# Fetching a quarter of the key rows through DRAM in the edge stage of a graph-attention and expert kernel

## The chip, the cores and the metric

The program runs on one core of a Trainium2 chip. The metric is the device time of one execution in microseconds (us). Before the change the median of three executions is 590.24 us (589.01 to 591.65). Engines are named as the profile names them: PE (TensorE), DVE (VectorE), ACT (ScalarE), POOL (GpSimd) and SP, whose queue issues plain transfers.

## The reference, cut to what matters

A layer norm, a Nystrom attention with a graph stage, and a mixture of 16 experts are computed in one launch. The change touches the graph stage alone:

```
enc = xg[0] + dense                      # only batch 0 is used: 512 tokens
q, k = enc @ wq, enc @ wk                # 32 columns each
scores = q @ k.T / sqrt(32)
contrib = adj_vals * scores[adj_rows, adj_cols]        # 16384 edges
A_raw = segment_sum(contrib, adj_rows, num_segments=n) # 512 sums
alpha = softmax(A_raw)
```

Since the score of an edge is a dot product, the kernel sums `adj_vals * k[adj_cols]` by row first (`kv` in the code), and multiplies by `q` afterwards.

## The kernel before, in words

The 16384 edges lie as 128 partitions by 128 columns, in 16 groups of 8 columns (`NG = 16`, `EG = 8`). One group takes these steps:

- VectorE makes a one-hot of the edges' columns (`one_hot_cols`, 4 instructions of 128x1024, L1204). TensorE gathers the key rows with it: 96 matmuls of 32 columns (`gather`, L2039), since `k` is held as three bf16 parts (`ksp`).
- VectorE multiplies the gathered rows in PSUM by the edge values (`product`, L1219). The result is split into three bf16 parts: ScalarE makes the first (`split_1`, L762), VectorE the residual (`middle`, L1226), ScalarE the second part (`split_2`, L766), VectorE the third (`lower`, L1231).
- The one-hot of the edges' rows is made by VectorE for 6 of 8 columns (`one_hot_rows`, L1212) and by ScalarE for 2 (`row_distances`, L773, and `last_rows`, L779).
- TensorE sums by row with 32 matmuls of 96 columns into bank 4 (`segment`, L2049).

Two slots (`s`) alternate between even and odd groups in all buffers. A loop runs 7 times over pairs of groups on PE, DVE and ACT; the last pair stands behind it. The order on each engine is the order in which the code is written, and semaphores join the engines. On DVE a group is product, one-hot of columns of the group two ahead, middle, one-hot of rows of the next group, lower. On ACT it is split_1, row_distances of the next group, split_2, last_rows of the next group. One-hot of rows for group g waits until segment g-2 has ended (`g_done`).

When the last segment has ended, a matmul of zeros (L2063) closes bank 4, VectorE forms the sums (L1255, L1258), the softmax follows, and SP starts the load of the experts' second weights. POOL does nothing in the edge stage: its last instruction before it is an iota (L551), its next waits for work far behind it. POOL is later the engine that gathers and scatters token rows for the experts, with indirect DMAs (`rows`, L602, and `results`, L610).

`kf` holds the key rows in fp32 in SBUF (L1193); L1194 to L1197 make `ksp` from it. `idx_i` and `idx_f` hold the edges' indices as integers and as floats.

Of the kernel before, what the change touches and what calls it, by code (L numbers as in the profile page):

```python
# [5 lines left out]
def sandwich_kernel(nc, dense, adj_rows, adj_cols, adj_vals, wq, wk, wv_w, wv_b, qkv_w, wq_t, wk_t, out_w, out_b,  # L6
                    conv_pad, keys_t, w1_t, b1_t, w2_t, b2, rw_t, rb, out):

    fp32 = mybir.dt.float32
# [23 lines left out]
    EG = 8  # L33
    EACT = 2
    NG = EC // EG
    QK = wq.shape[1]
    NS = 3
    E, TOPK = keys_t.shape[1], 4
# [25 lines left out]
    with ctx:  # L64
        def sb(name, shape, dt=fp32):
            return ctx.enter_context(nc.sbuf_tensor(name, shape, dt))
# [59 lines left out]
        colb = shared[:, 0:EDGE_OC].bitcast(fp16)  # L126
        oh_c = shared[:, EDGE_OC:EDGE_OR].bitcast(bf16).rearrange("p (a c n) -> p a c n", a=2, c=NT)
        oh_r = shared[:, EDGE_OR:EDGE_OR + EG * N].bitcast(bf16).rearrange("p (a j n) -> p a j n", a=2, j=EG)
        EDGE_OR1 = EDGE_OR + EG * N // 2
        qlT, klT = [shared[:, EDGE_OR1 + i * HP * B * L:EDGE_OR1 + (i + 1) * HP * B * L]  # L130
                    .rearrange("p (c n) -> p c n", c=HP) for i in range(2)]
# [42 lines left out]
        neg = sb("neg", [P, EC])  # L174
        vals = sb("vals", [P, EC])
        colT = sb("colT", [P, EC], fp16)
        col_dram = nc.dram_tensor("col_dram", [EDGES], fp16, kind="Internal").ap()

        kv, kvr = [xnT[:, i * N:(i + 1) * N].rearrange("p (a j q) -> p a j q", a=2, j=EG) for i in range(2)]
# [158 lines left out]

        def step_of(n):
            return n // JT * NI + n % JT

# [75 lines left out]
        def _(sp):  # L419
# [30 lines left out]
            sp.wait_ge(const_ready, 2)  # L450
            for i in range(BT):
                sp.dma_start(b2_bd[i * E:(i + 1) * E, i * D:(i + 1) * D], b2).then_inc(ffnc_in, 16)
            sp.wait_ge(alpha_ps, 1)
            sp.dma_start(w2_sb, w2_t).then_inc(w_in, 16)
            def store_rows(h):
# [31 lines left out]
            for i in range(IALL):  # L487
                if i == NI:
                    sp.wait_ge(exp_ready, 3)
                if first_of_group(i):  # L490
                    group = experts(sp, i)
                if i == 2:
                    sp.wait_ge(xg_in[1], 16)
                first_weights(i, group[i % NI % EB])
                if i == HOT_STEP + 12:
                    store_rows(1)
                elif i >= NI:
                    finish(i)
# [9 lines left out]
        def _(pool):  # L508
# [51 lines left out]
            iota(iota_x, [[1, P], [0, TK]], 0, 0).then_inc(const_ready, 1)  # L560


            pool.wait_ge(enc_ready, 1)
            for t in range(NT):
                if t == 0:
# [31 lines left out]
            def rows(n):  # L597
                if n >= XR:
                    pool.wait_ge(own_ready, 3 * ((n - XR) // GRP) + 1)
                if n >= XSEM:  # L600
                    pool.wait_ge(xg_in[n % XSEM], 16 * (n // XSEM))
                pool.indirect_dma_start(out=xg[:, n % XR, :], out_offset=None, in_=xd[n // JT][:, :],  # L602
                                        in_offset=bass.IndirectOffsetOnAxis(ap=idx_src[:, n:n + 1], axis=0))\
                    .then_inc(xg_in[n % XSEM], 16)
# [343 lines left out]
        def _(dve):  # L948
# [29 lines left out]
            def values(b):  # L978
                if b == 0:
                    dve.wait_ge(wv_in, 32)  # L980
                dve.wait_ge(val_ps, b + 1)
                v.tensor_tensor(out=value[:, b * NT:(b + 1) * NT, :],
                                in0=bank[2 + b % 2][:, :].rearrange("p (t d) -> p t d", t=NT),
                                in1=wvb_row[:, :].unsqueeze(1).broadcast_to([P, NT, D]), op=ALU.add)\
                 .then_inc(val_ready, 1)
# [18 lines left out]
            for b in range(1, 6):  # L1004
# [18 lines left out]
            step(v.tensor_tensor(out=idx_f[:, 1, :], in0=idx_f[:, 1, :], in1=neg[:, :], op=ALU.add))  # L1023
            v.tensor_scalar(idx_f[:, 1, :], idx_f[:, 1, :], 0.0, float(N - 1), ALU.max, ALU.min)\
             .then_inc(colT_need, 1)
            values(4)
            dve.wait_ge(xl_ps, 1)
            v.tensor_copy(xlT[:, :], bank[7][:, 0:B * L]).then_inc(xl_ready, 1)
# [184 lines left out]
                                          ALU.is_equal)  # L1213
                ins.then_inc(ohr_ready, 1)

            def product(pair, s):
                g = 2 * pair + s
                dve.wait_ge(kg_ps, 2 * pair + s + 3)
                v.tensor_tensor(out=kv[:, s, :, :],  # L1219
                                in0=bank[s][:, 0:EG * QK].rearrange("p (j q) -> p j q", j=EG),  # L1220
                                in1=vals[:, bass.ds(g * EG, EG)].unsqueeze(2).broadcast_to([P, EG, QK]),
                                op=ALU.mult).then_inc(kv_ready, 1)

# [18 lines left out]
                lower(pair, s)  # L1242

            dve.sem_inc(kv_ready, 2)
            with dve.Fori(0, NG // 2 - 1) as pair:
                group(pair, 0)
                group(pair, 1)
            group(NG // 2 - 1, 0, 1)
            group(NG // 2 - 1, 1, 0)
            enc(BH)  # L1250
            enc(BH + 1)

# [513 lines left out]
        def _(pe):  # L1766
# [285 lines left out]
                ins.then_inc(g_done, 1)  # L2052

            gather(0, 0)
            with pe.Fori(0, NG // 2 - 1) as pair:
                gather(pair, 1)
                segment(pair, 0)
                gather(pair + 1, 0)
                segment(pair, 1)
            gather(NG // 2 - 1, 1)  # L2060
            segment(NG // 2 - 1, 0)
            segment(NG // 2 - 1, 1)
            mm(bank[4][:, 0:NT * NS * QK], zeros[:, 0:P], zeros[:, 0:NT * NS * QK], start=False, stop=True,  # L2063
               skip_group_check=True).then_inc(alpha_ps, 1)
            idle(3, 7)
# [98 lines left out]
                    bias_rows(4 + (j - 4) // 2)  # L2164

            def rows_T(n):
                pe.wait_ge(xg_in[n % XSEM], 16 * (n // XSEM + 1))
                freed(pe, xgT_ready, n - 1)
                nc.tensor.transpose(bank[n % 2][:, 0:P], xg[:, n % XR, 0:D], ident[:, :]).then_inc(xgT_ps, 1)  # L2169

# [92 lines left out]
```

## Time and profile before

| | |
|---|---|
| median of three executions | 590.24 us |
| the profiled execution | 585.99 us, span 584.3 us |
| PE, DVE, ACT, POOL busy | 86%, 61%, 60%, 48% of the span |
| edge stage, first gather to last segment | 89.1 to 160.5 us |
| mean granted clock of TensorE | 0.929 of 2.4 GHz |

The profiled execution is 4.25 us below the median of the three timed ones, so sums over its rows are made against 585.99 us and their difference is then carried to 590.24 us. The span is the time between the first and last instruction. An engine's busy share over the whole span is a mean over stages with different limits: in the edge stage POOL is idle altogether.

### The profile page before, as it was taken

To read this page: it belongs to the slowest core of one execution; us is meant where nothing else is said; L and a number is where in the kernel's file an instruction comes from. 1 tells how busy PE (TensorE), PEld (TensorE's weight loads), DVE (VectorE), ACT (ScalarE), POOL (GpSimd) and SP (SyncE) were. 2 spreads that over 40 slices of the span, in tenths; PEclk is the share of its full clock that TensorE was granted. 3 is DMA by queue.
4 is the path that set the end of the run, shared out by engine and by line. 5 is a ranking of instruction groups with operands and counts; after the bars stand their busy time and mean duration, and the time that the engine had idled before them with its cause. 6 is when DMAs were issued, how large, how long until landed. Compare 5 with 4: busy or idle time off the path is not lost.

```text
span 584.3 us, 18669 instructions
## 1 busy us (share of the span) xinstructions
PE 501.3 (86%) x6226; PEld 464.5 (80%) x6226; DVE 354.3 (61%) x1302; ACT 353.1 (60%) x1067; POOL 282.4 (48%) x309
## 2 busy tenths in 40 slices
PE   3989978999826056999989999999999999999963
PEld 3975868999814043999989999999998999999722
DVE  6563666999889963667587787122235664442136
ACT  5723316777574643665686998666766666666404
POOL 5000010000005615776777777777777777777700
PEclk9999996999966557999999999999999999999978
DMA  8974000000070023675667776776698977687382
GB/s 242 255 228 191 3 3 3 0 0 0 1 288 1 1 90 107 189 204 167 176 182 188 196 264 177 206 215 182 178 269 268 288 227 199 201 234 225 101 289 74
DMA packets 55738, 92.19 MB, mean 158 GB/s; under 512 B 10352, under 2 KB 26096, under 8 KB 55152
## 3 DMA queue, kind: packets, MB, share of 16 engines
q1 hardware_dynamic: 45424, 72.35, 40.9%
q0 software_dynamic: 10240, 18.89, 11.4%
q8 instruction: 42, 0.69, 0.5%
q14 instruction: 32, 0.26, 0.2%
HBM read 78.07 MB, written 17.37 MB: 163 GB/s over the span
## 4 chain that ended last, share of the span: by engine, by line
PE 65%; DVE 15%; issue 6%; ACT 6%; DMA 4%; POOL 3%; DVEq 1%; POOLq 0%; SPq 0%; ACTq 0%
PE bank L2177 23%; PE bank L2184 21%; DVE shared L1212 3%; PE bank L2169 2%; DVE shared L1204 2%; PE bank L1771 2%; PE bank L2106 2%; DMA shared<-yd 2%; DMA yd<-value_early 2%; POOL yd L610 2%; PE bank L1876 2%; PE bank L1808 1%; PE bank L1798 1%; PE bank L2039 1%; PE bank L2122 1%
## 5 line engine op out<-in xcount | busy, mean ns | idle before, releaser
L908 ACT ACTIVATE value_early<-bank,shared 128x128 f32<-128x128 f32 x632 | 180.7, 369 | 96.8 <-PE bank L2177 95.4
L2177 PE MATMUL bank<-value_early,shared 128*128 x1264 | 170.2, 278 | 4.2 <-ACT value_early L916 3.6
L2184 PE MATMUL bank<-shared,value_early 128*128 x1264 | 167.4, 275 | 2.2 <-ACT value_early L908 2.2
L2177 PEld LDWEIGHTS bank<-value_early,shared 128*128 128x128 f32 x1264 | 154.9, 193 | 7.4 <-issue 7.3
L2184 PEld LDWEIGHTS bank<-shared,value_early 128*128 128x128 f32 x1264 | 154.0, 192 | 2.6 <-issue 2.6
L602 POOL DMA_INDIRECT shared<-xd,value_early x128 | 125.5, 980 | 56.1 <-issue 31.7
L610 POOL DMA_INDIRECT yd<-value_early x128 | 126.8, 991 | 40.6 <-issue 28.7
L1695 DVE SCALAR_TENSOR_TENSOR value_early<-bank,value_early 128x128 f32 x158 | 54.8, 347 | 88.5 <-PE bank L2184 76.1
L572 POOL TENSOR_TENSOR shared<-shared,xn 128x512 f32<-128x512 f32 x4 | 5.1, 1267 | 96.3 <-DVE xn L1288 89.9
L2039 PE MATMUL bank<-ksp,shared 128*128 128x32 bf16 x1536 | 41.1, 178 | 0.0
L2039 PEld LDWEIGHTS bank<-ksp,shared 128*128 128x128 bf16 x1536 | 40.3, 97 | 0.1
L551 POOL IOTA value_early<- 128x2048 f16 x1 | 2.5, 2466 | 73.6 <-PE bank L2014 73.6
L916 ACT ACTIVATE value_early<-bank 128x128 f32<-128x128 f32 x128 | 37.6, 295 | 0.3 <-PE bank L2169 0.3
L2169 PE MATMUL bank<-ident,shared 128*128 128x128 f32 x128 | 35.5, 277 | 1.7 <-DMA shared<-xd,value_early 1.7
L2049 PE MATMUL bank<-xnT,shared 128*128 128x96 bf16 x512 | 25.8, 211 | 7.1 <-DVE xnT L1231 7.1
L1777 PE MATMUL bank<-zeros 128*128 128x512 bf16 x55 | 16.4, 461 | 17.3 <-DVE mv L1297 12.2
L2049 PEld LDWEIGHTS bank<-xnT,shared 128*128 128x128 bf16 x512 | 23.8, 101 | 8.2 <-issue 5.4
L1777 PEld LDWEIGHTS bank<-zeros 128*128 128x128 bf16 x55 | 6.0, 112 | 25.7 <-DVE mv L1297 12.3
L1212 DVE TENSOR_SCALAR shared<-iota_r,idx_f 128x512 bf16<-128x512 f16 x90 | 24.9, 346 | 1.2 <-PE bank L2049 1.2
L1678 DVE TENSOR_TENSOR value_early<-shared,mask 128x128 f32<-128x128 f32 x16 | 4.7, 292 | 33.4 <-PE bank L2169 33.4
L1204 DVE TENSOR_SCALAR shared<-shared,iota_c 128x1024 bf16 x56 | 23.3, 478 | 0.0
L2169 PEld LDWEIGHTS bank<-ident,shared 128*128 128x128 f32 x128 | 18.5, 145 | 3.5 <-DMA shared<-xd,value_early 3.0
(341 smaller groups left out, 699.7 us busy)
## 6 DMA issues: line engine op xcount, KB each, us to landing
shared<-w1b SPq DMA_DIRECT2D x158, 258.0 KB
w1b<-in_w_t SPq DMA_DIRECT2D x1, 4096.0 KB
shared<-col_dram SPq DMA_DIRECT2D x1, 4096.0 KB
shared<-in_w_t SPq DMA_DIRECT2D x1, 4096.0 KB
att<-yd SPq DMA_DIRECT2D x8, 512.0 KB, 5.7
shared<-yd SPq DMA_DIRECT2D x4, 1024.0 KB, 9.1
xd<-xnT SPq DMA_DIRECT2D x2, 1280.0 KB, 5.1
shared<-xd,value_early POOLq DMA_INDIRECT x128, 3.7
```

The source lines that it names most:

```text
L602: pool.indirect_dma_start(out=xg[:, n % XR, :], out_offset=None, in_=xd[n // JT][:, :], in_offset=bass.IndirectOffsetOnAxis(ap=idx_src[:, ...
L610: pool.indirect_dma_start(out=yd[:, :], out_offset=bass.IndirectOffsetOnAxis(ap=idx_dst[:, m:m + 1], axis=0), in_=yg[:, m % YSLOTS, :], in ...
L908: ins = act.activation(hT[:, i % 2, tok(c)], bank[2 + i % 2][:, tok(c)], ACT.Gelu, bias=w1_now[:, i % WR, F + c:F + c + 1])
L916: act.activation(xgT[:, n % SLOTS, :], bank[n % 2][:, 0:P], ACT.Copy).then_inc(xgT_ready, 1)
L1204: ins = v.tensor_scalar(oh_c[:, s, c, :], colb[:, bass.ds(g * (EG * P), EG * P)], iota_c[:, c:c + 1], None, ALU.is_equal)
L1212: ins = v.tensor_scalar(oh_r[:, s, j, :], iota_r[:, :], idx_f[:, 0, bass.ds(g * EG + j, 1)], None, ALU.is_equal)
L1695: v.scalar_tensor_tensor(out=y, in0=bank[6 + i % 2][:, 0:P], scalar=own_f[:, bass.ds(own_at, 1)], in1=y, op0=ALU.mult, op1=ALU.add).then_i ...
L2039: ins = mm(bank[s][:, j * QK:(j + 1) * QK], oh_c[:, s, c, j * P:(j + 1) * P], ksp[:, c, n, :], start=(c == 0 and n == 0), stop=(c == NT - ...
L2049: ins = mm(bank[4][:, c * NS * QK:(c + 1) * NS * QK], oh_r[:, s, j, tok(c)], kvs[:, s, j, :, :].rearrange("p n q -> p (n q)"), start=False ...
L2169: nc.tensor.transpose(bank[n % 2][:, 0:P], xg[:, n % XR, 0:D], ident[:, :]).then_inc(xgT_ps, 1)
L2177: ins = mm(bank[2 + i % 2][:, tok(c)], w1_now[:, i % WR, tok(c)], x_now, start=True, stop=True)
L2184: ins = mm(bank[6 + i % 2][:, 0:D], hT[:, i % 2, tok(c)], w2_sb[:, bass.ds(e, 1), c, :] .rearrange("p a d -> p (a d)"), start=(c == 0), st ...
```

## The change

Four of the 16 groups (`GP = 4`, groups 12 to 15) no longer get their key rows from TensorE. SP stores `kf` to DRAM (`k_dram`), VectorE converts the clamped column indices to integers, and POOL issues 32 indirect DMAs, each of which fetches 128 rows of 128 bytes into `kgp`. The four one-hots of columns and the four gathers of these groups are gone. The loop runs 5 times instead of 7, and the groups behind it are written out, with the product of a group ahead of the lower part of the group before it. ScalarE's instructions are the same. The semaphores `xg_in[0]` to `xg_in[3]` are used for the 32 DMAs too, so later waits on them count 128 more (`landed`).

```diff
+    GP = 4
+    PP = (NG - GP) // 2
...
+        kgp = early[:, 0:GP * EG * QK].rearrange("p (a j q) -> p a j q", a=GP, j=EG)
...
+        def landed(n):
+            return xg_in[n % XSEM], 16 * (n // XSEM + 1) + (16 * EG if n % XSEM < GP else 0)
...
+            sp.wait_ge(ksp_ready, 1)
+            sp.dma_start(k_dram.rearrange("(c p) q -> p c q", p=P), kf[:, :, :]).then_inc(edge_in, 16)
             sp.wait_ge(alpha_ps, 1)
             sp.dma_start(w2_sb, w2_t).then_inc(w_in, 16)
...
+            pool.wait_ge(colT_need, 2)
+            pool.wait_ge(edge_in, 64)
+            for a in range(GP):
+                for j in range(EG):
+                    at = (NG - GP + a) * EG + j
+                    pool.indirect_dma_start(out=kgp[:, a, j, :], out_offset=None, in_=k_dram[:, :],
+                                            in_offset=bass.IndirectOffsetOnAxis(
+                                                ap=idx_i[:, 1, at:at + 1].bitcast(mybir.dt.uint32), axis=0))\
+                        .then_inc(xg_in[a], 16)
             pool.wait_ge(enc_ready, 1)
...
+            dve.wait_ge(colT_need, 1)
+            v.tensor_copy(idx_i[:, 1, :], idx_f[:, 1, :]).then_inc(colT_need, 1)
...
-            def product(pair, s):
+            def product(pair, s, fetched=None):
                 g = 2 * pair + s
-                dve.wait_ge(kg_ps, 2 * pair + s + 3)
-                v.tensor_tensor(out=kv[:, s, :, :],
-                                in0=bank[s][:, 0:EG * QK].rearrange("p (j q) -> p j q", j=EG),
+                if fetched is None:
+                    dve.wait_ge(kg_ps, 2 * pair + s + 3)
+                    rows = bank[s][:, 0:EG * QK].rearrange("p (j q) -> p j q", j=EG)
+                else:
+                    dve.wait_ge(xg_in[fetched], 16 * EG)
+                    rows = kgp[:, fetched, :, :]
+                v.tensor_tensor(out=kv[:, s, :, :], in0=rows,
...
-            with dve.Fori(0, NG // 2 - 1) as pair:
+            with dve.Fori(0, PP - 1) as pair:
                 group(pair, 0)
                 group(pair, 1)
-            group(NG // 2 - 1, 0, 1)
-            group(NG // 2 - 1, 1, 0)
+            group(PP - 1, 0, 1)
+            product(PP - 1, 1)
+            middle(PP - 1, 1)
+            for a in range(GP):
+                product(PP + a // 2, a % 2, a)
+                lower(PP - 1 + (a + 1) // 2, (a + 1) % 2)
+                one_hot_rows(PP + a // 2, a % 2)
+                middle(PP + a // 2, a % 2)
+            lower(NG // 2 - 1, 1)
...
-            with pe.Fori(0, NG // 2 - 1) as pair:
+            with pe.Fori(0, PP - 1) as pair:
...
-            gather(NG // 2 - 1, 1)
-            segment(NG // 2 - 1, 0)
-            segment(NG // 2 - 1, 1)
+            gather(PP - 1, 1)
+            for a in range(NG - 2 * PP + 2):
+                segment(PP - 1 + a // 2, a % 2)
```

On VectorE behind the loop, before the change (the last two groups; the lines are product, middle, one-hot of rows, lower):

```order
183 L1219 TENSOR_TENSOR xnT<-bank,vals 128x256
184 L1226 TENSOR_TENSOR xnT<-xnT 128x256
185 L1212 TENSOR_SCALAR shared<-iota_r,idx_f 128x512 x6
186 L1231 TENSOR_TENSOR xnT<-xnT 128x8x32
187 L1219 TENSOR_TENSOR xnT<-bank,vals 128x256
188 L1226 TENSOR_TENSOR xnT<-xnT 128x256
189 L1231 TENSOR_TENSOR xnT<-xnT 128x8x32
```

The same place with the change (groups 10, 11 and the start of 12 and 13; `value_early` is where `kgp` lies; L1244 is the product, L1250 middle, L1232 the one-hot of rows, L1255 lower):

```order
184 L1244 TENSOR_TENSOR xnT<-bank,vals 128x256
185 L1250 TENSOR_TENSOR xnT<-xnT 128x256
186 L1232 TENSOR_SCALAR shared<-iota_r,idx_f 128x512 x6
187 L1255 TENSOR_TENSOR xnT<-xnT 128x8x32
188 L1244 TENSOR_TENSOR xnT<-bank,vals 128x256
189 L1250 TENSOR_TENSOR xnT<-xnT 128x256
190 L1244 TENSOR_TENSOR xnT<-value_early,vals 128x256
191 L1255 TENSOR_TENSOR xnT<-xnT 128x8x32
192 L1232 TENSOR_SCALAR shared<-iota_r,idx_f 128x512 x6
193 L1250 TENSOR_TENSOR xnT<-xnT 128x256
194 L1244 TENSOR_TENSOR xnT<-value_early,vals 128x256
195 L1255 TENSOR_TENSOR xnT<-xnT 128x8x32
```

In a fetched group the one-hot of columns is gone, and the product stands ahead of the lower part of the group before.

On TensorE, before the change, from the end of the loop to the matmul of zeros that closes bank 4:

```order
108 L2049 MATMUL bank<-xnT,shared 128x96 x32
109 L2055 REGISTER_ALU
110 L2055 COMPARE_AND_BRANCH
111 L2039 MATMUL bank<-ksp,shared 128x32 x96
112 L2049 MATMUL bank<-xnT,shared 128x96 x64
113 L2063 MATMUL bank<-zeros 128x384
```

The same place with the change:

```order
108 L2080 MATMUL bank<-xnT,shared 128x96 x32
109 L2086 REGISTER_ALU
110 L2086 COMPARE_AND_BRANCH
111 L2070 MATMUL bank<-ksp,shared 128x32 x96
112 L2080 MATMUL bank<-xnT,shared 128x96 x192
113 L2094 MATMUL bank<-zeros 128x384
```

Behind the loop stand six segments instead of two, with no gather between them.

## Rows read from the trace of the kernel before

**Rows 1.** Busy time by stretch: PE, PEld, DVE, ACT, POOL, clock, DMA.

```profile
116.00:125.00 9.00, 8.37 (x279) 8.23 (x276) 8.96 (x28) 6.75 (x12) 0.00 (x0) 1.00 0.00 0
```

**Rows 2.** Timeline of one group: start, length, engine, line, count, idle before.

```profile
118.92 0.42 DVE L1219 TENSOR_TENSOR xnT<-bank,vals 128x256 f32<-128x256 f32 x1
119.03 1.52 PE L2049 MATMUL bank<-xnT,shared 128*128 128x96 bf16 x32 [0.25 <-DVE xnT L1231]
119.26 1.67 DVE L1204 TENSOR_SCALAR shared<-shared,iota_c 128x1024 bf16 x4
119.38 0.42 ACT L762 ACTIVATE xnT<-xnT 128x256 bf16<-128x256 f32 x1 [0.92 <-DVE xnT L1219]
119.70 1.32 ACT L773 ACTIVATE xnT<-iota_r,idx_f 128x512 f16<-128x512 f16 x2
120.39 2.55 PE L2039 MATMUL bank<-ksp,shared 128*128 128x32 bf16 x96
120.84 0.42 DVE L1226 TENSOR_TENSOR xnT<-xnT 128x256 f32<-128x256 f32 x1
121.18 1.66 DVE L1212 TENSOR_SCALAR shared<-iota_r,idx_f 128x512 bf16<-128x512 f16 x6
121.62 1.13 ACT L779 ACTIVATE shared<-xnT,ones 128x1024 bf16<-128x1024 f16 x1
```

**Rows 3.** Timeline: products of groups 11 and 15, and the closing matmul.

```profile
139.99 0.41 DVE L1219 TENSOR_TENSOR xnT<-bank,vals 128x256 f32<-128x256 f32 x1
...
156.78 0.42 DVE L1219 TENSOR_TENSOR xnT<-bank,vals 128x256 f32<-128x256 f32 x1 [0.39 <-PE bank L2039]
...
160.53 0.33 PE L2063 MATMUL bank<-zeros 128*128 128x384 bf16 x1
```

**Rows 4.** Timeline: the last instruction that makes the keys' parts.

```profile
88.64 0.29 DVE L1197 TENSOR_TENSOR ksp<-kres,ksp 128x128 bf16<-128x128 f32 x1
```

**Rows 5.** DMA issues (size, us to landing); SP's waits (total, times, longest).

```profile
idx_i<-in_adj_rows SPq DMA_DIRECT2D x1, 64.0 KB, 5.8
SPq L454 <- PE bank L2063: 116.9, 1, 116.9
```

**Rows 6.** Line L602, POOL's gathers: ns min/median/max, and time to landing.

```profile
L602 POOL DMA_INDIRECT shared<-xd,value_early x128: 942/947/2028, 223.9 to 498.3; - x128
...
DMA to landing us min/median/max: 3.1/3.7/5.7
```

**Rows 7.** Timeline of DVE, then POOL, around two gathers.

```profile
342.25 1.22 DVE L1457 TENSOR_TENSOR att<-place,att 128x1024 bf16<-128x1024 f32 x1
...
342.60 1.68 POOL L602 DMA_INDIRECT shared<-xd,value_early  x1 [0.30 <-issue]
344.58 0.95 POOL L602 DMA_INDIRECT shared<-xd,value_early  x1 [0.30 <-issue]
```

**Rows 8.** Timeline of DVE, then POOL: trains of three short VectorE instructions.

```profile
348.53 1.02 DVE L1502 TENSOR_SCALAR xnT<-iota_r,att,code 128x128 f16<-128x128 f16 x3
349.21 0.42 DVE L1495 TENSOR_TENSOR xnT<-iota_r,att 128x256 f16<-128x256 f16 x1
351.79 0.76 DVE L1502 TENSOR_SCALAR xnT<-iota_r,att,code 128x128 f16<-128x128 f16 x3
352.46 0.41 DVE L1495 TENSOR_TENSOR xnT<-iota_r,att 128x256 f16<-128x256 f16 x1
...
348.58 0.97 POOL L610 DMA_INDIRECT yd<-value_early  x1 [0.30 <-issue]
```

**Rows 9.** Busy time by stretch (columns as in rows 1), the first two groups.

```profile
92.20:95.60 3.40, 2.25 (x91) 2.15 (x86) 3.40 (x11) 2.67 (x5) 0.00 (x0) 0.99 0.02 5
95.60:102.40 6.80, 5.80 (x138) 5.83 (x139) 5.48 (x18) 3.64 (x6) 0.00 (x0) 0.50 0.01 2
```

**Rows 10.** Timeline of PE: the segment of group 0.

```profile
96.60 2.72 PE L2049 MATMUL bank<-xnT,shared 128*128 128x96 bf16 x32 [2.15 <-DVE xnT L1231]
```

**Rows 11.** Line L1021: VectorE's conversion of the indices, ns min/median/max.

```profile
L1021 DVE CAST idx_f<-idx_i x1: 282/282/282, 27.2 to 27.2; 128x256 f32<-128x256 int32 x1
```

More of the change, by code:

```diff
@@ L176, in sandwich_kernel @@
         colT = sb("colT", [P, EC], fp16)
+        k_dram = nc.dram_tensor("k_dram", [N, QK], fp32, kind="Internal").ap()
         col_dram = nc.dram_tensor("col_dram", [EDGES], fp16, kind="Internal").ap()
@@ L492, in _ @@
                 if i == 2:
-                    sp.wait_ge(xg_in[1], 16)
+                    sp.wait_ge(*landed(1))
                 first_weights(i, group[i % NI % EB])
@@ L600, in rows @@
                 if n >= XSEM:
-                    pool.wait_ge(xg_in[n % XSEM], 16 * (n // XSEM))
+                    pool.wait_ge(*landed(n - XSEM))
                 pool.indirect_dma_start(out=xg[:, n % XR, :], out_offset=None, in_=xd[n // JT][:, :],
@@ L2166, in rows_T @@
             def rows_T(n):
-                pe.wait_ge(xg_in[n % XSEM], 16 * (n // XSEM + 1))
+                pe.wait_ge(*landed(n))
                 freed(pe, xgT_ready, n - 1)
```

## The prediction

> **What bounds the kernel now.** I looked first at the busy time by stretch inside the edge stage [rows 1]. In 9.00 us of the loop VectorE is busy 8.96, TensorE 8.37, ScalarE 6.75, POOL 0, at the full clock. So VectorE is the bound, TensorE is 0.6 us behind it, and POOL and the DMA rings are free. The timeline of one group then gives the terms [rows 2]: on VectorE a product of 0.42, four one-hots of columns that take 1.67, a middle of 0.42, six one-hots of rows that take 1.66, and a lower of about 0.42; a successor starts 0.34 after a start of 0.42 length, and 1.58 after the start of a block of one-hots. The period is (156.78 - 139.99)/4 = 4.20 us [rows 3]. TensorE needs a segment of 1.52 and a gather of 2.55 in it. Last I read the first two groups, since the clock is not full there [rows 9].
>
> **What is taken away.** Four gathers of 2.55 us and 16 one-hots of columns go. I count from the product of group 11, at 139.99 us. Before the change the closing matmul starts at 160.53, 20.54 us later [rows 3]. With the change the rest of the stage has ScalarE as its bound, because its work per group is unchanged: split_1 to row_distances 0.32, row_distances 1.32, split_2 to last_rows about 0.33, last_rows 1.13 [rows 2], together 3.1. VectorE needs only 0.34 + 0.34 + 1.58 + 0.34 = 2.6 per group, TensorE 1.52. Laid out: split_1 of group 11 starts 0.46 after its product (119.38 - 118.92), split_1 of group 15 at 0.46 + 4 x 3.1 = 12.9. In each group lower waits for the second split; lower of group 14 starts 0.32 + 1.32 + 0.42 + 0.05 = 2.1 after its split_1, so at 9.8 + 2.1 = 11.9. Behind it come the one-hots of rows, and middle of group 15 starts at 11.9 + 0.34 + 1.58 = 13.8. From there middle, split_2 and lower follow with 0.45 each, 0.1 to the segment, and 1.36 from the segment to the closing matmul: 13.8 + 1.35 + 0.1 + 1.36 = 16.6. The saving is 20.5 - 16.6 = 3.9 us. The product ahead of lower is part of this: it fills the wait of lower for the second split, which ends 0.05 us before it.
>
> **What is added off the path.** The store of the keys waits for the keys' last part, which ends at 88.93 [rows 4]. SP has nothing ahead of it: it waits 116.9 us for TensorE in this time [rows 5], and its next transfer, the second weights, goes out only at the end of the stage. A 64 KB transfer landed after 5.8 us in a crowded stretch [rows 5], so POOL starts at about 94.5 at the latest. VectorE's conversion costs one instruction of at most 0.28 us [rows 11]; it stands where the chain of waits runs on TensorE, and would cost 0.3 if it were not hidden. I take 0. Behind the 32 DMAs on POOL stands only work that waits for the end of the softmax. The changed counts of the expert gathers' semaphores add no instruction: 0.
>
> **Are the rows there in time?** One gather of POOL takes 0.947 us and 0.30 pass before the next [rows 6, 7]: a pitch of 1.25, so 32 x 1.25 = 40 us. A gather can be held up: the one of 1.68 us runs beside an instruction with two inputs in SBUF, L1457, which ends at 343.47; the gather ends 0.81 after that [rows 7]. In the loop VectorE is never idle, so I estimate 1.4 per gather: 94.5 + 45 = 139.5, and 3.7 to landing [rows 6] makes 143. The product of group 15 needs them at 139.99 + 10.9 = 150.9. The pitch may reach (150.9 - 3.7 - 94.5)/32 = 1.65 us before group 15 waits. The earlier groups have more room.
>
> **What POOL does to VectorE.** The trace of before has no gather beside the dense one-hots, so this is bounded. The train of short scalar compares at 348.53 is 1.02 us long, where the one at 351.79 is 0.76; the longer one ends at 349.55, exactly where POOL's DMA ends (348.58 + 0.97) [rows 8]. So the end of POOL's instruction holds back a write of VectorE by up to 0.26 us. But the instruction behind the train starts 0.68 after the train's start in one case and 0.67 in the other [rows 8]: nothing was lost. That is the lower bound, 0. The upper bound is 0.26 per gather. The nearest rows are short instructions with a pause in each; the one-hots are longer. From the blocks of 1.67/4 = 0.42 (1024 elements) and 1.66/6 = 0.28 (512 elements) [rows 2], 512 elements cost 0.14, so 0.14 of each instruction is a pause that swallows part of the hold: 0.26 - 0.14 = 0.12 lost when it strikes. The one-hots are 3.2 of 4.2 us, which makes 0.09, and since the nearest rows show none I take 0.08. Between 95.60 and 102.40 VectorE is busy 5.48 of 6.80 [rows 9], so the 6 gathers up to there are free, and 26 x 0.08 = 2.1 us are lost (bounds 0 and 26 x 0.26 = 6.8).
>
> The Trainium skill, page "SBUF — State Buffer", section "SBUF: two separate sides", says that VectorE in its two-port modes and GpSimd share a port pair by an exclusive lock, held for the whole instruction, and that GpSimd's descriptor writing starves meanwhile; the same page gives about 620 ns alone against about 3100 ns beside a VectorE copy. By the 3100 ns, an estimate from that page, the 32 gathers would take 99 us and come some 40 us late. The trace agrees that there is a lock, at the end of POOL's instruction, but not with "whole instruction": trains run within POOL's 0.97 us [rows 8].
>
> **TensorE's clock behind the loop.** With 1.52 us of work in 3.1, TensorE is busy half of the time. In the stretch 92.20 to 95.60 it was busy 2.25 of 3.40, and the clock fell to half for the next 6.8 us [rows 9]. There the segment took 2.72 us instead of 1.52 [rows 10, 2]. I expect this fall in the last four groups. The other segments hide it, since 2.72 is under 3.1; the last one is on the path: +1.2 us. Without the fall it is 0.
>
> **Sum.** -3.9 + 2.1 + 1.2 = -0.6 us. The profiled execution of 585.99 becomes 585.4. The median of the runs shown is 4.25 above it, so the forecast is 590.24 - 0.6 = 589.6. What lies behind the stage is a chain on VectorE and ScalarE that moves as a whole.
>
> **The rivals.**
> - *The gathers cost nothing.* VectorE swallows the hold as in the trains [rows 8]. Then -3.9 + 1.2 = -2.7 with the fall of the clock, -3.9 without it: 587.5 to 586.3. For it: the next start was on time. Against it: the one-hots leave a smaller pause. If what POOL takes is under 0.03 per gather and the clock holds, it is a gain of over 3 us.
> - *The whole hold is lost, and the loop's TensorE falls to the lower clock.* VectorE loses 0.26 at each of 26 gathers, 6.8 us, with the clock's 1.2: -3.9 + 6.8 + 1.2 = +4.1, 594.3. A period of 4.46 instead of 4.20 also leaves TensorE idle longer, and each fall in the loop costs at least the 1.2 us of a segment [rows 10, 2]. It is slower than before from 0.11 us per gather on. For it: the lock is there, and VectorE has no spare time. Against it: the starts in the trains.
> - *POOL is starved and the rows come late.* It gets through only about once per group, in the product, which reads PSUM. By 141 us some 11 of 32 are done; group 13 waits, and the remaining 21 go at about 1.3 behind the loop: 141 + 27 + 3.7 = 172, then 5.7 from the product of group 15 to the end, 178 against 160.5: +17, 607. It decides from a pitch of 1.65. That the change doesn't do what it says is this case. Against it: POOL's DMA was not lengthened by the train [rows 8]. By the page of the Trainium skill named above it would come out later still, as said there.
>
> **How the numbers follow.** Forecast (a loss between 0.03 and 0.2 per gather) 0.45, gathers free 0.30, whole hold 0.16, starved 0.09. I take 0.5%, 3 us, as what a measurement of this kernel can tell from no change. Faster by more than that: 0.25 of the free case (where the clock holds too, or a little more is won behind it) and 0.07 of the forecast: 0.32. Slower by more: 0.13 of the whole hold, 0.09, and 0.03 of the forecast: 0.25. Within it: 0.43. The range reaches from the free case, 586.3 less 1.0 for the spread of the medians, to the whole hold with one fall in the loop, 594.3 + 1.2: 585.3 to 595.5. It leaves out the starved case. The likeliest case alone has 587 to 593.
>
> **What would show it.** 32 DMAs on POOL between 92 and 143 us with a pitch of 1.25 to 1.5; the product of group 11 later than 139.99 by some 2 us; no wait of a fetched product for POOL or a DMA; a spacing of 3.1 between the last products, with ScalarE without idle time; a granted clock of half in the last groups, and the last segment at 2.7 us. The forecast is wrong if the product of group 11 stays at 140, if the fetched products wait for DMAs, or if POOL's instructions last over 1.5 us.

## The result, and the profile after

The changed kernel has a median of 583.56 us (582.05 to 584.30, four executions), the kernel before 589.83 beside it. The ratio is 0.9886, 95% interval 0.9854 to 0.9919: faster by 6.3 us (1.1%, clear of 1), and outside the predicted range of 585.3 to 595.5. Run twice more unchanged, it gave 0.9966 [0.9922, 1.001] and 0.9945 [0.9905, 0.9984]. Weighted by their intervals the three make 0.992, about 4.5 us; the first number was on the lucky side.

The gain is in the edge stage. I measure it from the start of the product of group 0, P0, to the start of the matmul that closes bank 4, "close". In before that is 92.20 to 160.53 [rows 3]; in the profiled execution after it is 95.07 to 158.98:

| kernel | P0 to close | P1 to P2 | P3 to P10 | P11 to close |
|---|---|---|---|---|
| before | 68.33 | 5.65 | 29.64 | 20.53 |
| before, again | 68.35 | 5.65 | 29.66 | 20.54 |
| after | 63.91 | 4.85 | 30.24 | 15.81 |
| after, again | 63.51 | 4.30 | 30.43 | 15.81 |
| after, third | 63.34 | 4.61 | 30.24 | 15.82 |

Here Pg is the start of the product of group g in us (of L1244 after, L1219 before). The stage is 4.42 us shorter in the pair of profiles: the tail gives 4.72, the steady loop costs 0.60, the first groups give 0.30. The tail repeats to 0.01 us. The spans differ by only 2.0 (584.3 and 582.3), since P0 stands 2.87 later after the change for a reason that is not the change (last section), and 0.4 is won behind the stage, where I looked for no cause.

Page of after, parts 1 and 5 (part 5: line, engine, names, count | busy us, mean ns | idle before, and what ended it):

```profile
span 582.3 us, 17846 instructions
PE 494.1 (85%) x5840; PEld 457.1 (79%) x5842; DVE 350.1 (60%) x1287; ACT 351.8 (60%) x1067; POOL 316.2 (54%) x341
L577 POOL DMA_INDIRECT value_early<-k_dram,idx_i x32 | 34.9, 1090 | 15.1 <-issue 9.4
```

POOL's 32 gathers are there, 1.09 us each. Two stretches of after, busy us of PE, PEld, DVE, ACT, POOL, then the granted clock, in the columns of [rows 1]:

```profile
113.00:122.00 9.00, 7.89 (x258) 7.78 (x259) 9.00 (x28) 6.20 (x10) 6.97 (x7) 1.00 0.15 12
144.40:155.90 11.50, 5.75 (x125) 5.33 (x123) 10.12 (x36) 11.15 (x20) 0.00 (x0) 1.00 0.01 1
```

The first answers to [rows 1]: VectorE is still never idle, and POOL is now busy 6.97 of 9.00. The second lies in the fetched groups: ScalarE is busy 11.15 of 11.50, and TensorE only half of the time, 5.75, at the full clock. Timeline of after (start, duration, engine, line; in brackets what the instruction waited for), answering to [rows 3]:

```profile
143.16 0.42 DVE L1244 TENSOR_TENSOR xnT<-bank,vals 128x256 f32<-128x256 f32 x1 [0.39 <-PE bank L2070]
153.61 0.42 DVE L1244 TENSOR_TENSOR xnT<-value_early,vals 128x256 f32<-128x256 f32 x1
157.62 1.52 PE L2080 MATMUL bank<-xnT,shared 128*128 128x96 bf16 x32 [1.30 <-DVE xnT L1255]
158.98 0.33 PE L2094 MATMUL bank<-zeros 128*128 128x384 bf16 x1
```

From the product of group 11 to the closing matmul it is 15.8 us, where before it was 20.5. The last segment is 1.52 long, not 2.72 as in [rows 10]. One fetched group of the same timeline, which answers to [rows 2]:

```profile
147.52 0.42 DVE L1250 TENSOR_TENSOR xnT<-xnT 128x256 f32<-128x256 f32 x1
147.85 0.42 DVE L1244 TENSOR_TENSOR xnT<-value_early,vals 128x256 f32<-128x256 f32 x1
148.05 0.40 ACT L784 ACTIVATE xnT<-xnT 128x256 bf16<-128x256 f32 x1
148.35 1.13 ACT L797 ACTIVATE shared<-xnT,ones 128x1024 bf16<-128x1024 f16 x1
148.48 0.43 DVE L1255 TENSOR_TENSOR xnT<-xnT 128x256 bf16<-128x256 f32 x1 [0.21 <-ACT xnT L784]
148.82 1.66 DVE L1232 TENSOR_SCALAR shared<-iota_r,idx_f 128x512 bf16<-128x512 f16 x6
149.05 1.52 PE L2080 MATMUL bank<-xnT,shared 128*128 128x96 bf16 x32 [1.36 <-DVE xnT L1255]
149.39 0.40 ACT L780 ACTIVATE xnT<-xnT 128x256 bf16<-128x256 f32 x1
149.70 1.32 ACT L791 ACTIVATE xnT<-iota_r,idx_f 128x512 f16<-128x512 f16 x2
150.40 0.42 DVE L1250 TENSOR_TENSOR xnT<-xnT 128x256 f32<-128x256 f32 x1
150.73 0.42 DVE L1244 TENSOR_TENSOR xnT<-value_early,vals 128x256 f32<-128x256 f32 x1
150.92 0.40 ACT L784 ACTIVATE xnT<-xnT 128x256 bf16<-128x256 f32 x1
```

Product to product is 150.73 - 147.85 = 2.88. ScalarE starts split_2 at 148.05, last_rows 0.30 later, split_1 1.04 later, row_distances 0.31 later, and the next split_2 1.22 after that, together 2.87, without a pause between them. VectorE has a ring that is nearly as long: middle, split_2, lower, one-hot of rows, middle (150.40 - 147.52 = 2.88 here). In group 15, where ScalarE is free, middle, split_2 and lower start at 156.15, 156.60 and 157.05, 0.45 apart; so by itself this ring would take 0.45 + 0.45 + 0.34 + 1.58 = 2.82, and ScalarE's 2.87 is the bound by 0.05. No fetched product waits for a DMA.

Last, the loop, where POOL works beside VectorE. Timeline of after:

```profile
91.83 0.40 SPq L461 DMA_DIRECT2D k_dram<-kf  x1
94.53 1.11 POOL L577 DMA_INDIRECT value_early<-k_dram,idx_i  x1 [5.70 <-DMA k_dram<-kf]
114.73 1.52 POOL L577 DMA_INDIRECT value_early<-k_dram,idx_i  x1 [0.30 <-issue]
115.36 1.79 DVE L1232 TENSOR_SCALAR shared<-iota_r,idx_f 128x512 bf16<-128x512 f16 x6
132.66 1.92 DVE L1232 TENSOR_SCALAR shared<-iota_r,idx_f 128x512 bf16<-128x512 f16 x6
137.54 1.31 POOL L577 DMA_INDIRECT value_early<-k_dram,idx_i  x1 [0.30 <-issue]
```

The store lands 2.7 us after its issue and POOL starts at 94.53; the last of 32 goes at 137.54, a pitch of (137.54 - 94.53)/31 = 1.39 us. A block of six one-hots of rows takes 1.79 or 1.92 where it took 1.66 [rows 2]: one or two of its instructions lost 0.13.

### The profile page after: what moved, and what is told of

Its sections match the earlier page's. It is cut to its first block, busy times and chain, and to the rows that moved or that the text cites. A ratio compares the mean times of both kernels' runs of the same rounds, so it can differ in the third digit from the quotient of the medians.

```text
span 582.3 us, 17846 instructions
## 1 busy us (share of the span) xinstructions
PE 494.1 (85%) x5840; PEld 457.1 (79%) x5842; DVE 350.1 (60%) x1287; ACT 351.8 (60%) x1067; POOL 316.2 (54%) x341
## 4 chain that ended last, share of the span: by engine, by line
PE 68%; DVE 14%; ACT 7%; issue 5%; DMA 3%; POOL 2%; DVEq 1%; POOLq 0%; SPq 0%; ACTq 0%
PE bank L2208 24%; PE bank L2215 22%; PE bank L2200 2%; DVE shared L1232 2%; PE bank L1802 2%; PE bank L2153 2%; PE bank L2137 2%; PE bank L1839 2%; DMA shared<-yd 2%; DVE shared L1224 2%; PE bank L1829 2%; PE bank L1907 2%; POOL yd L628 1%; PE bank L2070 1%; PE bank L2004 1%
## 5 line engine op out<-in xcount | busy, mean ns | idle before, releaser
L577 POOL DMA_INDIRECT value_early<-k_dram,idx_i x32 | 34.9, 1090 | 15.1 <-issue 9.4
L2080 PE MATMUL bank<-xnT,shared 128*128 128x96 bf16 x512 | 24.6, 207 | 13.1 <-DVE xnT L1255 13.1
L2070 PE MATMUL bank<-ksp,shared 128*128 128x32 bf16 x1152 | 31.3, 179 | 0.0
L2070 PEld LDWEIGHTS bank<-ksp,shared 128*128 128x128 bf16 x1152 | 30.6, 98 | 0.3
L1232 DVE TENSOR_SCALAR shared<-iota_r,idx_f 128x512 bf16<-128x512 f16 x90 | 26.2, 359 | 0.4 <-PE bank L2080 0.4
L791 ACT ACTIVATE xnT<-iota_r,idx_f 128x512 f16<-128x512 f16 x32 | 21.1, 707 | 0.0
```

The lines of the kernel that those rows point to most:

```text
L577: pool.indirect_dma_start(out=kgp[:, a, j, :], out_offset=None, in_=k_dram[:, :], in_offset=bass.IndirectOffsetOnAxis(ap=idx_i[:, 1, at:at ...
L1232: ins = v.tensor_scalar(oh_r[:, s, j, :], iota_r[:, :], idx_f[:, 0, bass.ds(g * EG + j, 1)], None, ALU.is_equal)
L2070: ins = mm(bank[s][:, j * QK:(j + 1) * QK], oh_c[:, s, c, j * P:(j + 1) * P], ksp[:, c, n, :], start=(c == 0 and n == 0), stop=(c == NT - ...
L2080: ins = mm(bank[4][:, c * NS * QK:(c + 1) * NS * QK], oh_r[:, s, j, tok(c)], kvs[:, s, j, :, :].rearrange("p n q -> p (n q)"), start=False ...
```

## The experiments

### POOL's part alone, and the order alone

Theory: the tail's gain comes from ScalarE's bound and POOL takes far less than 0.08 per gather. Rival: the gain has another source, and POOL's price is as forecast. The first kernel keeps the store, the conversion and the 32 gathers, and gets its groups from TensorE as before:

```diff
-            with dve.Fori(0, PP - 1) as pair:
+            with dve.Fori(0, NG // 2 - 1) as pair:
...
             for a in range(GP):
-                product(PP + a // 2, a % 2, a)
...
+                dve.wait_ge(xg_in[a], 16 * EG)
+            group(NG // 2 - 1, 0, 1)
+            group(NG // 2 - 1, 1, 0)
```

> The kernel before with POOL's part of the change alone: the store of the keys, the conversion of the indices and the 32 gathers into a buffer that nobody reads; TensorE gathers all 16 groups as before. Theory (the hold is small): POOL's gathers lengthen a group of the loop from 4.20 to about 4.30 us while they run, so 0.6 to 0.9 us in all, and the edge stage from the keys' last part (L1197 of before) to the closing matmul is 71.9 + 0.8 = 72.7 us. Rival (my forecast: 0.08 per gather): +2.1, 74.0 us. Second rival (whole hold of 0.26): +6.8, 78.7 us.

Measured: 1.0025 [0.9986, 1.0064]; P0 to close 69.49 against 68.33 at the same P1 to P2 (5.64), so POOL's part costs 1.16 us, 0.036 per gather. That is more than the 0.6 to 0.9 of the theory and about half of the 2.1 of my forecast. P3 to P10 is 30.50 (+0.86); the tail, where POOL is done, is 20.54 and unchanged.

The second keeps everything but the order of the fetched groups:

```diff
-                product(PP + a // 2, a % 2, a)
-                lower(PP - 1 + (a + 1) // 2, (a + 1) % 2)
                 one_hot_rows(PP + a // 2, a % 2)
+                lower(PP - 1 + (a + 1) // 2, (a + 1) % 2)
+                product(PP + a // 2, a % 2, a)
                 middle(PP + a // 2, a % 2)
```

> The changed kernel with the order of the parts in the fetched groups as before: one-hot of rows of the next group, lower, then the next product, then middle. Theory (in the fetched groups two chains are equally long, ScalarE's own work of 2.87 us, and middle, second split, lower, one-hot of rows): with the old order product, first split and middle stand in a row, 0.34 + 0.13 + 0.47 + 0.34 + 1.58 + 0.34 = 3.2 us per group instead of 2.87, so from the product of group 11 to the closing matmul 16.6 to 17.2 us instead of 15.8: the kernel is 0.8 to 1.4 us slower than the changed one. Rival (ScalarE alone sets the period, the order is worth nothing): 15.8 us again.

Measured: 0.9983 [0.9944, 1.0023], tail 19.28. The expectation, 3.2 us per group and 16.6 to 17.2, missed: a group takes 3.70. Timeline of this kernel:

```profile
148.25 0.42 DVE L1255 TENSOR_TENSOR xnT<-xnT 128x256 bf16<-128x256 f32 x1
148.81 1.52 PE L2080 MATMUL bank<-xnT,shared 128*128 128x96 bf16 x32 [2.18 <-DVE xnT L1255]
150.37 1.67 DVE L1232 TENSOR_SCALAR shared<-iota_r,idx_f 128x512 bf16<-128x512 f16 x6 [0.46 <-PE bank L2080]
151.95 0.42 DVE L1255 TENSOR_TENSOR xnT<-xnT 128x256 bf16<-128x256 f32 x1
158.37 2.67 PE L2080 MATMUL bank<-xnT,shared 128*128 128x96 bf16 x32 [0.48 <-DVE xnT L1255]
160.88 0.33 PE L2094 MATMUL bank<-zeros 128*128 128x384 bf16 x1
```

Here is a ring that I had not seen: lower of a group releases its segment, the segment's end (`g_done`) releases the one-hot of rows of the group two ahead, since that buffer has two slots, and the next lower stands behind these one-hots on VectorE. 0.56 + 1.56 + 1.58 = 3.70. Fetching the rows without the order gives 20.53 - 19.28 = 1.3 us; the order gives 19.28 - 15.81 = 3.5.

The 3.5 is not the ring alone. The last segment takes 2.67 us here and 1.52 in the changed kernel: TensorE's clock fell during the last group. The granted clock is 0.97 from 152.52 to 157.70, with TensorE busy 3.00 of 5.18, and 0.50 from there to the closing matmul. From the start of the last segment to that matmul it is 160.88 - 158.37 = 2.51, in the changed kernel 158.98 - 157.62 = 1.36. So 1.15 of the 3.5 is the clock, and 2.3 is what the ring costs up to the last segment.

### The changed kernel again

> The changed kernel once more, in five rounds. Theory (what is won lies in the edge stage: 4.7 us behind the product of group 11, less 0.6 for POOL in the loop, and up to 1.2 from where TensorE's clock falls ahead of the loop): 4.1 to 5.3 us less than before, ratio 0.991 to 0.993, and the prologue of the trace moves by up to 4 us from one execution to the next with the time at which the clock first rises. Rival (something outside the edge stage is won too): the ratio stays at 0.9886, 6.7 us.

Measured: 585.47 us, 0.9966 [0.9922, 1.001], stage 63.51, tail 15.81. The stage repeats; the time of the whole execution does not repeat as well.

### The rows by plain transfers

POOL's 32 gathers are taken out and SP issues 32 plain transfers of the same size into `kgp`. The rows are then not the edges' rows, so this kernel computes something else in the four groups.

```diff
-            for a in range(GP):
-                for j in range(EG):
-                    pool.indirect_dma_start(out=kgp[:, a, j, :], ...
+                    sp.dma_start(kgp[:, a, j, :],
+                                 k_dram.rearrange("(c p) q -> p c q", p=P)[:, j % NT, :])
```

> The changed kernel with POOL's 32 gathers replaced by 32 plain transfers on SP's queue of the same size, which bring the key rows of the tokens in order and not those of the edges; VectorE waits for all of them ahead of the first fetched product. Theory (hold small): the loop falls back to 4.20 us per group, and the kernel is 0.6 to 0.9 us faster than the changed one, with the same 15.8 us from the product of group 11 to the closing matmul. Rival (my forecast): 2.1 us faster than the changed one. Second rival (a plain transfer disturbs the loop as much): the same time.

Measured: 0.9954 [0.9918, 0.999]; P0 to close 63.51 with P1 to P2 at 5.65, P3 to P10 29.54. The 63.51 is 68.33 less the tail's 4.72, to 0.1 us. So without POOL the loop loses nothing. Lines of VectorE in P3 to P10, first in the kernel with POOL's gathers alone (count | busy us, mean ns | idle), then with plain transfers:

```profile
L1232 DVE TENSOR_SCALAR shared<-iota_r,idx_f 128x512 bf16<-128x512 f16 x42 | 12.7, 367 | 0.0
L1224 DVE TENSOR_SCALAR shared<-shared,iota_c 128x1024 bf16 x28 | 11.7, 477 | 0.0
```

```profile
L1220 DVE TENSOR_SCALAR shared<-shared,iota_c 128x1024 bf16 x28 | 11.6, 479 | 0.0
L1228 DVE TENSOR_SCALAR shared<-iota_r,idx_f 128x512 bf16<-128x512 f16 x42 | 11.6, 347 | 0.0
```

The one-hots of rows lose 20 ns in the mean and the longer one-hots of columns, in the mean, nothing. 42 x 0.020 = 0.84 us, most of the 0.96 by which P3 to P10 differs.

### How many groups to fetch

`GP` is changed to 5, 2 and 6. For 5 the groups ahead of the fetched ones are written for an even number in the loop:

```diff
-    GP = 4
+    GP = 5
...
-            group(PP - 1, 0, 1)
-            product(PP - 1, 1)
-            middle(PP - 1, 1)
+            group(PP - 1, 0)
+            group(PP - 1, 1, 1)
+            product(PP, 0)
+            middle(PP, 0)
```

> The changed kernel with five fetched groups (40 gathers) instead of four. Theory (a fetched group costs 2.88 us instead of 4.20, a gather costs VectorE 0.03 to 0.04 us, POOL needs 1.38 us per gather): POOL ends some 55 us after its start, the rows of the last group land about 1 us after they are wanted, and the edge stage from the product of group 0 to the closing matmul is 63.0 to 63.8 us instead of 63.5 to 63.9: 0 to 0.9 us less than the changed kernel. Rival (POOL's gathers still hold VectorE for 0.08 each and the rows come more than 2 us late): 64.5 us or more.

> The changed kernel with two fetched groups (16 gathers). Theory: from the product of group 13 to the closing matmul 10.1 us instead of 12.1 before the change, and 0.5 us lost to 16 gathers: the edge stage from the product of group 0 to the closing matmul is 66.4 to 67.0 us, between the 68.3 of before and the 63.9 with four. Rival (the gain comes once, from the new order of the last groups, and not per group): near 64.5 us with two groups already.

> The changed kernel with six fetched groups (48 gathers). Theory (POOL's pitch of 1.38 us sets when rows are there): the last rows land some 69 us after POOL's start, 12 us later than wanted; VectorE waits for DMAs at the last products, and the stage from the product of group 0 to the closing matmul is 72 to 75 us, 4 to 7 us slower than the kernel before. Rival (POOL speeds up to 1.25 as soon as VectorE waits, and the rows come only some 8 us late): 69 to 70 us.

Measured, with four groups beside them:

| groups | ratio | P0 to close | at P1 to P2 of |
|---|---|---|---|
| 2 | 0.9970 [0.9937, 1.0004] | 66.61 | 5.65 |
| 4 | (three ratios above) | 64.77, worked out | 5.65 |
| 5 | 0.9958 [0.9922, 0.9994] | 63.56 | 5.65 |
| 6 | 1.0033 [0.9996, 1.0071] | 69.58 | 5.64 |

The 64.77 is 68.33 + 1.16 - 4.72, since every profile of the four-group kernel had a shorter P1 to P2. Two and five groups came out as expected. With six the rows come late; the product of group 15 in its timeline:

```profile
155.96 0.42 DVE L1244 TENSOR_TENSOR xnT<-value_early,vals 128x256 f32<-128x256 f32 x1 [6.85 <-DMA value_early<-k_dram,idx_i]
```

It waits 6.85 us for POOL's transfers. My figure for this was 72 to 75; the 69 to 70 of the rival was right, but not for its reason. POOL's 48 gathers took from 91.07 to 153.18, 1.32 each: up to the one at 126.75 the pitch is 1.37, from there on 1.26, and all but one of these later gathers take 0.94 to 0.96 us. VectorE does not merely wait in this time: it is busy 15.82 of the 18.00 us from 131 to 149. What is over near 127 is the one-hots of columns.

### Early product, but the one-hots of rows ahead of lower

This tells the ring from the product's place. The product stays early; only lower moves behind the one-hots:

```diff
                 product(PP + a // 2, a % 2, a)
-                lower(PP - 1 + (a + 1) // 2, (a + 1) % 2)
                 one_hot_rows(PP + a // 2, a % 2)
+                lower(PP - 1 + (a + 1) // 2, (a + 1) % 2)
                 middle(PP + a // 2, a % 2)
```

> The changed kernel with the one-hot of rows of a fetched group ahead of the lower part of the group before (product, one-hot of rows, lower, middle). Theory (the one-hot buffer of two slots closes a ring: lower, segment, then the one-hot of rows two groups on): with this order the ring is lower 0.42 + 0.14, segment 1.52, one-hot of rows 1.58 and the semaphores' 0.05, 3.70 us per group as in the run with the old order, so 18.5 to 19.3 us from the product of group 11 to the closing matmul instead of 15.8. Rival (ScalarE's 2.87 us per group is the only bound): 15.8 us again. What the place of the product alone is worth is the difference to the old order, near zero by the theory, 3.4 us by the rival.

Measured: 0.9962 [0.9924, 0.9999], tail 18.92, inside the 18.5 to 19.3 of the ring. Timeline of this kernel:

```profile
148.79 0.42 DVE L1255 TENSOR_TENSOR xnT<-xnT 128x256 bf16<-128x256 f32 x1
149.35 1.52 PE L2080 MATMUL bank<-xnT,shared 128*128 128x96 bf16 x32 [2.18 <-DVE xnT L1255]
150.91 1.67 DVE L1232 TENSOR_SCALAR shared<-iota_r,idx_f 128x512 bf16<-128x512 f16 x6 [1.03 <-PE bank L2080]
152.49 0.41 DVE L1255 TENSOR_TENSOR xnT<-xnT 128x256 bf16<-128x256 f32 x1
```

The period is 3.70 again, although the product is early. So the 3.1 us (18.92 - 15.81) come from the place of lower, which here stands behind the one-hots of rows, and these wait for a segment. Of the 3.1 again a part is the clock: the last two segments, 64 matmuls without a pause, take 4.08 us, from 156.76 to the closing matmul at 160.84, with a granted clock of 0.64. At the 1.36 that 32 of them need in the changed kernel it would be 2.72. By this estimate the clock is 1.4 and the ring 1.7 of the 3.1. Lower ahead of them without the early product was not tried.

### The kernels once more, side by side

The kernel before, unchanged, and the changed kernels with four and five groups ran again on one chip:

> The kernel before against itself, for a second trace and for what such a comparison can tell. Theory (executions of one kernel differ by the time at which TensorE's clock first rises, and by its state in the first groups of the loop): ratio 1 within 0.004, the edge stage from the product of group 0 to the closing matmul 68.3 us with a slow second group of 5.65 us, or 67.0 without one, and the product of group 0 anywhere between 91.6 and 97.8 us. Rival (before has a fixed prologue, and the change moves it): the product of group 0 at 92.2 again.

> The changed kernel a third time, on one chip with five fetched groups. Theory: 3.5 us less than before at the same clock in the first groups, 4.4 to 4.8 where the clock is the better one, so ratio 0.992 to 0.994; the edge stage 63.5 to 64.9 us. Rival (the first comparison was right): 0.9886.

> Five fetched groups again, beside the changed kernel. Theory: the edge stage is 1.2 us shorter than the changed kernel's at the same clock in the first groups (63.6 us with a slow second group), so ratio 0.990 to 0.992, about 0.002 under the changed kernel's. Rival (the fifth group's rows come late in other executions): the same ratio as the changed kernel.

Measured: before 0.9993 [0.9956, 1.0030]; four groups 0.9945 [0.9905, 0.9984]; five groups 0.9923 [0.9889, 0.9956]. The stage is 68.35, 63.34 and 62.45. Five groups is the best version by the stage, 64.77 - 63.56 = 1.2 us at one clock pattern and 0.9 side by side (P1 to P2 4.61 and 4.70); the intervals of the whole times overlap, so as a time this is not shown.

### Does TensorE's clock hold?

In the changed kernel, with TensorE at 1.52 of 2.88 us, it held to the end of the stage. In the two kernels with a period of 3.70 it fell in the last group, at about 157.7 us, behind groups in which TensorE was busy 1.52 of 3.70. Here the segments of the fetched groups have half of their matmuls (the output leaves out the other half of those edges):

```diff
-                segment(PP - 1 + a // 2, a % 2)
+                segment(PP - 1 + a // 2, a % 2, EG if a < 2 else EG // 2)
```

> The changed kernel with half of the matmuls (16 of 32) in the segments of the four fetched groups; the sums of the last four groups lack half of their edges. Theory (the clock stayed up since TensorE's 1.52 us in 2.88 is enough work): with 0.8 us in 2.88 the clock falls to half in the last groups, and the remaining segments take 1.3 us or more instead of 0.76; the stage then ends about where it does now. Rival (the clock looks only at pauses, and none is over 2.1 us): the clock stays up to 160 us, segments 0.76, and the stage is 0.7 us shorter.

Measured, one execution: 584.18 us, tail 15.70. Timeline of the segments of its four fetched groups:

```profile
148.53 0.84 PE L2080 MATMUL bank<-xnT,shared 128*128 128x96 bf16 x16 [1.36 <-DVE xnT L1255]
151.41 1.28 PE L2080 MATMUL bank<-xnT,shared 128*128 128x96 bf16 x16 [2.04 <-DVE xnT L1255]
154.28 1.44 PE L2080 MATMUL bank<-xnT,shared 128*128 128x96 bf16 x16 [1.60 <-DVE xnT L1255]
157.10 1.44 PE L2080 MATMUL bank<-xnT,shared 128*128 128x96 bf16 x16 [1.38 <-DVE xnT L1255]
```

Sixteen matmuls take 0.84 and then 1.44 us: the granted clock is 1.00 from 148.53 to 151.40, where TensorE is busy 0.84 of 2.87, and 0.50 from 154.28 on (1.2 of 2.4 GHz). So a fall as forecast came here, in the one execution that was run. The tail hardly gains: the last segment, which is on the path to the closing matmul, has half of the matmuls at half of the clock and takes 1.44 us instead of 1.52. The segments before it are not on the path.

## Why the prediction was wrong

The forecast was -0.6 us; by the stage at one clock pattern it is 64.77 - 68.33 = -3.6, by the timed ratios -4.5. Of all cases the rival in which the gathers cost nothing and the clock holds (-3.9) was nearest. Term by term:

- **The tail, -3.9 forecast, -4.7 measured.** The mechanism was right in its main part: the rest of the stage has a bound of ScalarE, and the product ahead of lower fills the wait for split_2. The size was off, since I counted row_distances and last_rows by their durations, 1.32 and 1.13 [rows 2]; back to back the next instruction starts 1.22 and 1.04 after them. I had made this very correction for VectorE (0.34 for a length of 0.42) and left it out for ScalarE. With 0.33 for 0.30 the four make 3.10 instead of 2.87. Three such periods and one more row_distances lie on the path that I laid out, 3 x 0.23 + 0.10 = 0.8 us, and the tail came out at 15.8 where 16.6 was forecast. I spoke of the product's place as a part of this gain; the order as a whole is 3.5 of the 4.7 us, with 1.15 of it the clock that the old order loses. Lower behind the one-hots of rows closes a ring through the two slots of the one-hot buffer, which the prediction did not name.
- **What POOL takes, +2.1 forecast, +1.2 measured.** This step failed by its size: 0.036 per gather, not 0.08, inside its bounds. In the loop the longer one-hots of columns lost nothing in the mean, 477 ns against 479, although I had counted both kinds alike. Where an instruction was hit it mostly lost 0.13 or 0.14, close to the estimate (0.12), but in the kernel with POOL's part alone only 11 of the 174 one-hots of rows took more than 400 ns, so most of the 32 gathers cost nothing at all. The rival of the whole hold, 0.26 per gather, falls.
- **The clock, +1.2 forecast, 0 measured.** This step failed outright for the changed kernel: the last segment took 1.52, not 2.72. I carried over one stretch, busy 2.25 of 3.40 [rows 9], and took half-busy for the cause of the fall. That one stretch does not carry it: in the second profile of the changed kernel TensorE is also busy 2.25 of 3.40 from 93.15 to 96.55, and the granted clock is 1.00 there and stays 1.00 up to 101.77. With 5.75 of 11.50 in the fetched groups it stayed at 2.4 GHz too. The price was right: with 1.52 of work in 3.70 the clock did fall, and cost 1.15 us at the end. What made it fall at 95.60 before is open.
- **The rows in time.** Right in its outcome: the pitch was 1.39 (1.4), the last gather started at 137.54 and no product waited. That POOL started at 94.53, where 94.5 was forecast, is luck: the keys' last part came 2.9 later than in before, and the store landed 2.7 us after its issue, not 5.8. In the kernel with POOL's part alone POOL started at 92.33. With six groups the other side of the limit showed. The starved rival falls. The Trainium skill, page "SBUF — State Buffer", section "SBUF: two separate sides", has the lock held for the whole instruction and 3100 ns for GpSimd beside a VectorE copy. Beside one-hots that never pause the gathers took 0.94 to 1.52 us, so the 3100 ns did not come, and no one-hot of rows was lengthened by more than about 0.2 us, so POOL did not hold VectorE back for a whole gather. Whether VectorE holds POOL back for a whole one-hot is not decided by these numbers. My estimate by the 3100 ns of the Trainium skill, some 40 us late, should have read 94.5 + 99 + 3.7 - 150.9 = 46.
- **Store and conversion, 0.** No cost was seen: the kernel with six groups, which has both, had its P0 at 91.61, earlier than before's 92.20. They were not tried alone, and the scatter of P0 would hide 0.3 us.
- **The range.** -4.7 + 1.2 gives -3.5, which by the median of before would have been 586.7 and inside the range. The 583.56 outside it contains a shorter clock dip in the first groups, 0.8 us in the profiled execution, and some luck of the draw: the next two comparisons gave -2.0 and -3.2 us. I allowed 1.0 for the spread of the medians, where executions of one kernel here spread over 10 us.

Which of the signs that I named came true: the 32 DMAs with a pitch of 1.39, no wait for a DMA and ScalarE without idle time did; a spacing of 3.1 and a clock of half did not. Single gathers reached 1.52 us, just over the 1.5 that I had named as a sign of being wrong; it meant nothing, since the pitch held. The product of group 11 stands at 143.16, 3.2 later than 139.99, but only because P0 is 2.9 later; an absolute time was a bad sign to name, where P3 to P10 would have told it.

## What to carry to other kernels

When work is taken from a pipeline, look for what then closes a ring: here two slots of a buffer and the order of the instructions on VectorE, with the fall of the clock that came with the longer period, were worth 3.5 us, the removed matmuls and one-hots without it only 1.3. A bound for an engine is the sum of the distances between starts where it works back to back; the sum of the durations is too long, here by 0.2 in 3.1 us. In a comparison of single profiles, measure from one anchor to another inside the stage, and at the same clock: the tail repeated to 0.01 us, while whole executions differed by several.

## What the hardware showed that I had not expected

**The clock's first rise moves.** Executions of the same kernel spread from about 583 to 593 us. In the profiles TensorE's clock first rises at 20.4, 24.5, 29.1 or 33.0 us. Timeline of PE in before, then in its repetition (each row is eight matmuls of one kind):

```profile
22.36 0.96 PE L1808 MATMUL bank<-blk_l,xn 128*128 128x8 f32 x8
```

```profile
24.11 1.71 PE L1808 MATMUL bank<-blk_l,xn 128*128 128x8 f32 x8
32.65 1.14 PE L1808 MATMUL bank<-blk_l,xn 128*128 128x8 f32 x8
35.05 0.96 PE L1808 MATMUL bank<-blk_l,xn 128*128 128x8 f32 x8
```

At 22.36 the one has the full clock (0.96 us for eight), the other still has half of it at 24.11 (1.71); there the clock rises within the row at 32.65, and only then eight take 0.96. P0 follows at 92.20 and at 97.78, and the spans are 584.3 and 590.7: the same kernel, 5.6 us apart before the stage begins. Two more profiles with a rise at 33.0, one with two groups and one with five, have their P0 at 97.78 and 97.72. After has its rise at 29.1 and its P0 at 95.07, so the profiled pair shows too little of the gain. What decides the rise was not tried.

**The dip in the first groups.** P1 to P2 is 5.65 us in nine of the fourteen profiles and 4.30 to 4.86 in the others, also between two executions of the kernel with five groups (5.65 and 4.70), and both kernels that differ from after only by the order behind group 10 had 5.65. The granted clock between P1 and P2 is 0.50 where it takes 5.65 (before), 0.65 where it takes 4.86 (after), and 1.00 where it takes 4.31 (after, again). It goes with the first rise: all five profiles with a rise at 20.4 or 33.0 have the long one, all four at 29.1 a short one, and at 24.5 there are four long and one short. So it is the clock's, and it moves the stage by up to 1.3 us. All profiles of the changed kernel happened to have a short one and both of before a long one; that the change has no part in this is likely by the kernel with five groups, not shown for the one with four.

**POOL's gathers and VectorE's dense one-hots lengthen each other little.** The gathers took 940 to 1519 ns beside them. Source line of after (min/median/max ns):

```profile
L577 POOL DMA_INDIRECT value_early<-k_dram,idx_i x32: 940/1022/1519, 94.5 to 137.5; - x32
L1232 DVE TENSOR_SCALAR shared<-iota_r,idx_f x90: 332/344/544, 97.3 to 155.9; 128x512 bf16<-128x512 f16 x90
```

VectorE's longest one-hot of rows took 544 where the median is 344, and half of POOL's gathers were within 82 ns of the shortest. The one-hots of columns are spared in the mean only: their median in after is 475 ns, but one of the 40 on this line took 695. With six groups POOL's gathers were shortest once the one-hots of columns were over. Why the two kinds of one-hot differ is not settled.
